# First tile of an attention and low-rank feed-forward block: q's norms wholly on TensorE, v's Gram matrix between q's products, v's low parts ahead of the later scales

## The chip, the cores and the metric

The kernel runs on one core of one Trainium2 chip. The metric is the device time of one launch in microseconds (us). The time before is the median of 3 runs.

## What is computed

x is 4096 rows of 1024 float32. The block is a pre-norm attention whose 32 heads attend to each other within one row, and a feed-forward layer with a low-rank expert part:

```python
q = (layernorm(x) @ wq.T + bq).reshape(B, S, H, D)      # k and v alike; H = D = 32
probs = softmax(einsum('bshd,bstd->bsht', q, k) / sqrt(D))   # 32 x 32 per row
x = x + einsum('bsht,bstd->bshd', probs, v).reshape(B, S, E)
y = layernorm(x)
w_full = softmax of the 2 largest of y @ gate_w.T, on 8 experts
low = einsum('bsd,erd->ebsr', y, lora_A)                 # rank 16
x = x + y @ base_w.T + base_b + 2 * einsum('ebsr,eor,bse->bso', low, lora_B, w_full)
```

All weights are float32 arrays of 1024 x 1024; wq, wk and wv hold values that fp8 can hold. Rows are independent of each other.

## The kernel before

The rows go through in 32 tiles of 128. Every float32 operand of a large product is cut into two float16 parts: the high part is the scaled value rounded to float16, the low part is what is left. A product then is three matmuls (high times high, low rows times high weights, high rows times low weights). From the second tile on, a flag says whether the low parts of k, q and v are zero and the third matmul is left out.

Scaling needs a power of two for each weight matrix before it can be cut. It comes from a norm of the whole matrix: `gram` multiplies each 128-wide column block of each chunk (128 rows of the transposed weight) with itself on TensorE, in bfloat16, 8 matmuls a chunk and 64 a matrix, and adds them up in one PSUM bank. `norm_diag` (VectorE) takes the diagonal, `spread_norm` (TensorE) sums it over the partitions into all of them by a product with ones, and `scale` (VectorE) makes the scale from it in a few instructions of one column. Then `high_parts` (ScalarE, one 128x1024 instruction a chunk) writes the high parts and `split` (VectorE, one a chunk, L1059) the low parts. `attention_scale` and `attention_undo` are short chains on VectorE that need the scales.

In the first tile all of this is interleaved with the tile's own work, in an order written out by hand for each engine:

- SyncE queues the loads: tile 0's rows, the eight chunks of k, the eight of q, k's bias, tile 1's rows, the eight chunks of v (each waits for the low part of the same chunk of k, whose place it takes), the other biases, the expert matrices `ag`, lora_B and the eight chunks of base. q is staged where v's parts will lie, so v's high and low parts wait for the last low part of q.
- TensorE (`first_step`): two chunks of q's Gram matrix, then k's products chunk by chunk (`project_chunk`: 6 matmuls of 512 columns, each waiting for its low part), with one chunk of q's Gram matrix after each of the first three. Only 5 chunks of q go this way (`GRAM_CHUNKS`). `spread_norm("q")` stands before k's last chunk. Then v's Gram matrix, q's products, the Gram matrices of ag, lora and base, the squares of k's low parts, the spreads of these norms, v's products, and the scores (`attend`).
- ScalarE: the high parts of k, the square sums of q's chunks 5 to 7 (`q_norms`, L704), k's bias, the high parts of q, the high part of k's turned rows, the square sums of four low parts of k (`low_part_norms`), the statistics of tile 1's rows, v's high parts 0 to 3, the high part of q's turned rows, v's high parts 4 to 7, `gate_high` (high parts of ag), `normalise_quads(1)` (tile 1's rows are scaled), base's first high parts.
- VectorE: k's low parts, q's scale, q's low parts 0 and 1, the bias adds of k (`add_bias`, L1196, which empty the PSUM banks), `turn_first` (k's rows transposed, L1356), v's scale, q's low parts 2 to 7, `first_low`, v's low part 0, the bias adds of q, `turn_second` (L1369), the diagonals and scales of ag, lora and base, v's low parts 1 to 7, `gate_split`, `turn_quads(1)` (tile 1's rows transposed, L1225), and then the bias adds of v, `turn_third`, `shift` (softmax's maximum) and so on.
- GpSimd: `row_root(1)` (five one-column operations), `second_lo(0)` (low part of q's turned rows, 128x1024, L626), `zero_diag` (four memsets of staged chunks that v's low parts have freed), `v_low(0)` (L632). SyncE spreads k's turned parts into the zeroed diagonal blocks (`first_hi`, `first_lo`).

The engines meet only through semaphores, and each runs its own list in order. Two orders matter for the change: a `norm_diag` on VectorE stands still until the Gram matrix is complete on TensorE, and whatever is behind it in VectorE's list stands with it; and a `project_chunk` on TensorE stands until its low part is there.

Of the kernel before, what the change touches and what calls it, by code (L numbers as in the profile page):

```python
# [69 lines left out]
def block_kernel(nc, x, wT, agT, lora_b, biases, out):  # L70
    T = x.shape[0] // P
    with ExitStack() as ctx:
# [124 lines left out]
        GRAM_CHUNKS = {"k": KC, "q": 5, "v": KC, "ag": KC, "base": KC, "lora": KC}  # L197
# [58 lines left out]
        q_squares = sem("q_squares")  # L256
# [185 lines left out]
        def _(sp):  # L442
# [46 lines left out]
            def first_hi(t):  # L489

                sp.wait_ge(a_hi_ready, t + 1)
                if t > 0:

                    sp.wait_ge(ctx_acc, t)
                else:

                    sp.wait_ge(diag_zero, block_diag_len // HID)
                spread_k(0, t)

            def first_lo(t):  # L500

                sp.wait_ge(a_lo_ready, t + 1)
                spread_k(1, t)
# [196 lines left out]
        def _(act):  # L700
# [5 lines left out]
            def q_norms():  # L706

                for i, k in enumerate(range(GRAM_CHUNKS[SECOND], KC)):
                    act.wait_ge(w_loaded[SECOND][k], 16)
                    if i > 0:  # L710
                        act.wait_ge(q_squares, i)
                    square_sum_of(staged[SECOND][k], norm_in[SECOND][:, P + i:P + i + 1]).then_inc(q_squares, 1)

            def low_part_norms():

                for k in range(LOW_BY_ACT):
                    act.wait_ge(w_lo_done[FIRST], k + 1)
                    act.wait_ge(q_squares, KC - GRAM_CHUNKS[SECOND])
# [67 lines left out]
            q_norms()  # L786
# [53 lines left out]
            def first_step():  # L840
# [3 lines left out]
                low_part_norms()  # L844
# [7 lines left out]
                high_parts("v", w_hi["v"], KC // 2, KC)  # L852
                gate_high()
                normalise_quads(1)
# [134 lines left out]
        def _(dve):  # L989
# [268 lines left out]
            split(FIRST, w_hi[FIRST], w_lo[FIRST], KC - 2, KC)  # L1258
            scale(SECOND)
            attention_scale(1, SECOND)  # L1260
# [160 lines left out]
            def first_step():  # L1421
# [3 lines left out]
                add_bias(0, 1, FIRST, 1, a_acc, a_biased)  # L1425
                norm_diag("v")
                turn_first(0)
# [3 lines left out]
                split(SECOND, w_hi[SECOND], w_lo[SECOND], 2, KC)  # L1431
# [6 lines left out]
                turn_second(0)  # L1438
                norm_diag("ag")
                norm_diag("lora")  # L1440
                norm_diag("base")
                scale("ag")
                scale("lora")
                base_scale()
                split("v", w_hi["v"], w_lo["v"], 1, KC)
# [171 lines left out]
        def _(pe):  # L1617
# [81 lines left out]
            def spread_norm(g):  # L1699

                pe.wait_ge(norm_diags, SCALED.index(g) + 1)
                if GRAM_CHUNKS[g] < KC:

                    pe.wait_ge(q_squares, KC - GRAM_CHUNKS[g])
# [151 lines left out]
            def first_step():  # L1856
# [12 lines left out]
                for k in range(KC):  # L1869
                    if k == KC - 1:  # L1870
                        spread_norm(SECOND)
                    project_chunk(FIRST, k, (0, 1), a_acc)
                    if k + 2 < GRAM_CHUNKS[SECOND]:
# [191 lines left out]
```

## Time and profile before

| | us |
|---|---|
| median of 3 runs | 1277.32 (1276.88 to 1278.81) |
| the profiled execution | 1278.39 |
| its span, first to last instruction | 1275.3 |
| outside the span | 3.1 |
| TensorE busy | 1242.0 (97%) |
| VectorE busy | 1067.5 (84%) |
| ScalarE busy | 743.3 (58%) |
| GpSimd busy | 426.5 (33%) |

The page's 40 slices of 32 us show TensorE at 6, 8 and 9 tenths in the first three and at 9 nearly everywhere after. In the rows, a line gives the start in us from the start of the span, the length in us, the engine, the line of the kernel, the operation, what it writes and reads, and how many instructions are merged; in square brackets stands how long the engine was idle before it and what ended that. PE is TensorE, DVE is VectorE, ACT is ScalarE, POOL is GpSimd. Instructions of one engine overlap a little at their ends, so a merged row's length over its count is close to the distance from one to the next.

### The profile page before, as it was taken

Reading aid. Unit: us, or ns where it says so; the run is one execution under the profiler, and the core shown is the slowest. Engines: PE = TensorE matmul, PEld = TensorE weight load, DVE = VectorE, ACT = ScalarE, POOL = GpSimd, SP = SyncE. Lnnn points to the kernel's source line nnn. Section 1 sums busy time; section 2 is a strip of 40 time slices with the busy share of each in tenths; the row PEclk is TensorE's granted clock in tenths of the full one; section 3 lists DMA queues with packets and bytes.
Section 4 is the critical chain, followed back from the end, with each engine's and each line's share of the span. In section 5 each row is a group of like instructions: output and inputs, shape, how many; then the busy total and the mean of one; then the engine's idle time right before and its main releaser. Section 6 shows DMA issues by size and latency. Waiting matters only on the chain.

```text
span 1275.3 us, 30571 instructions
## 1 busy us (share of the span) xinstructions
PE 1242.0 (97%) x12314; PEld 642.1 (50%) x12314; DVE 1067.5 (84%) x1492; ACT 743.3 (58%) x1149; POOL 426.5 (33%) x340
## 2 busy tenths in 40 slices
PE   6899989999999999999999999999999999999998
PEld 4554445455554545455454555545455555545454
DVE  5799898888888888888888888888888888888886
ACT  4876646665556666555666655566665556666431
POOL 0113433334423333442333344233334423333320
PEclk9999999999999999999999999999999999999999
DMA  9823543344444334444433444443344444333330
GB/s 367 295 67 85 133 100 92 89 101 115 101 96 97 96 84 101 115 101 97 97 96 84 102 115 101 97 96 96 84 103 115 99 98 96 96 84 87 85 84 33
DMA packets 295447, 136.41 MB, mean 107 GB/s; under 512 B 265072, under 2 KB 266096, under 8 KB 295408
## 3 DMA queue, kind: packets, MB, share of 16 engines
q1 hardware_dynamic: 228688, 112.28, 33.6%
q10 hardware_dynamic: 66720, 23.60, 7.8%
q8 instruction: 26, 0.43, 0.1%
q14 instruction: 13, 0.11, 0.0%
HBM read 86.03 MB, written 33.03 MB: 93 GB/s over the span
## 4 chain that ended last, share of the span: by engine, by line
PE 84%; DVE 7%; DMA 3%; issue 2%; ACT 2%; SPq 1%; POOL 0%; DVEq 0%; ACTq 0%
PE acc L1630 23%; PE dense_acc L1790 23%; PE acc L1639 22%; PE attn_ps L1732 7%; PE dense_acc L1800 2%; DMA work<-wT_dram 2%; PE low_ps L1769 1%; PE low_ps L1762 1%; PE low_ps L1763 1%; PE dense_acc L1805 1%; DMA turn_dram<-x_turned 1%; DVE w_lo_k L1059 1%; ACT work L401 1%; DVE work L1196 1%; DVE work L1157 1%
## 5 line engine op out<-in xcount | busy, mean ns | idle before, releaser
L1790 PE MATMUL dense_acc<-base_parts,x 128*128 128x512 f16 x1488 | 331.2, 380 | 1.1 <-issue 1.0
L401 ACT COPY work<-work 32x512 f16<-32x512 f16 x498 | 306.5, 615 | 12.4 <-PE attn_ps L1732 0.3
L1790 PEld LDWEIGHTS dense_acc<-base_parts,x 128*128 128x128 f16 x1488 | 145.7, 99 | 165.6 <-issue 2.2
L632 POOL TENSOR_TENSOR work<-work 128x1024 f16<-128x1024 f32 x32 | 68.4, 2137 | 225.9 <-ACT work L917 225.9
L1196 DVE SCALAR_TENSOR_TENSOR work<-acc,acc_to_a,biases_sb 128x512 f32<-128x512 f32 x192 | 136.3, 738 | 1.8
L582 POOL TENSOR_TENSOR columns<-columns 128x1 f32<-128x1 f32 x31 | 9.1, 293 | 362.9 <-ACT work L797 362.9
L763 ACT CAST x_hi<-x_turned 128x1024 f16<-128x1024 f32 x31 | 32.4, 1044 | 155.3 <-PE acc L1639 154.4
L1630 PE MATMUL acc<-w_hi_k,x_hi 128*128 128x512 f16 x496 | 117.5, 380 | 1.6 <-issue 1.6
L1630 PE MATMUL acc<-v_parts,x_hi 128*128 128x512 f16 x496 | 117.5, 380 | 0.0
L1639 PE MATMUL acc<-w_hi_k,x_lo 128*128 128x512 f16 x496 | 117.2, 379 | 0.0
L1630 PE MATMUL acc<-w_hi_q,x_hi 128*128 128x512 f16 x496 | 117.2, 379 | 0.0
L1639 PE MATMUL acc<-w_hi_q,x_lo 128*128 128x512 f16 x496 | 117.2, 379 | 0.0
L1639 PE MATMUL acc<-v_parts,x_lo 128*128 128x512 f16 x496 | 117.2, 379 | 0.0
L626 POOL TENSOR_TENSOR work<-work 128x1024 f16<-128x1024 f32 x32 | 97.4, 3044 | 47.5 <-ACT work L910 43.5
L1732 PEld LDWEIGHTS attn_ps<-work 128*32 128x32 f16 x6144 | 86.4, 97 | 30.2 <-issue 26.4
L1732 PE MATMUL attn_ps<-work 128*32 128x128 f16 x6144 | 97.5, 220 | 2.9 <-DVE work L1418 1.7
L1307 DVE SCALAR_TENSOR_TENSOR work<-dense_acc,w_undo_bits,work 128x512 f32<-128x512 f32 x64 | 45.2, 747 | 51.7 <-PE dense_acc L1805 48.2
L825 ACT ACTIVATE columns<-columns 128x1 f32<-128x1 f32 x32 | 6.5, 203 | 135.8 <-issue 92.5
L645 POOL TENSOR_TENSOR work<-work,biases_sb 128x1024 f32<-128x1024 f32 x32 | 75.6, 2363 | 17.6 <-DMA out_dram<-work 15.1
L1314 DVE STREAM_TRANSPOSE work<-attn_ps 128x1024 f32<-128x1024 f32 x32 | 63.2, 1975 | 19.4 <-PE attn_ps L1732 19.3
L1639 PEld LDWEIGHTS acc<-w_hi_k,x_lo 128*128 128x128 f16 x496 | 48.4, 98 | 58.8 <-issue 0.5
L1639 PEld LDWEIGHTS acc<-v_parts,x_lo 128*128 128x128 f16 x496 | 48.5, 98 | 58.6
(217 smaller groups left out, 2070.1 us busy)
## 6 DMA issues: line engine op xcount, KB each, us to landing
work<-x_dram SPq DMA_DIRECT2D x64, 512.0 KB, 3.6
work<-work SPq DMA_DIRECT2D x256, 64.0 KB, 2.0
work<-x_dram SPq DMA_DIRECT2D x124, 128.0 KB, 3.8
out_dram<-work SPq DMA_DIRECT2D x31, 512.0 KB, 2.6
x_turned<-turn_dram ACTq DMA_DIRECT2D x30, 512.0 KB, 3.3
work<-wT_dram SPq DMA_DIRECT2D x16, 512.0 KB, 9.9
turn_dram<-x_turned SPq DMA_DIRECT2D x64, 128.0 KB, 3.9
turn_dram<-x_turned ACTq DMA_DIRECT2D x60, 128.0 KB, 4.4
```

Source lines behind the costliest of these rows:

```text
L401: copy(diag[c * QD:(c + 1) * QD, :, c, j::NQ, :], src).then_inc(vdiag_ready, 1)
L626: nc.gpsimd.tensor_tensor(dense_parts[:, :, 1, :], kq_rows(t), dense_parts[:, :, 0, :], ALU.subtract).then_inc(b_lo_ready, 1)
L632: nc.gpsimd.tensor_tensor(v_parts_t[:, :, 1, :], turned3, v_parts_t[:, :, 0, :], ALU.subtract).then_inc(v_lo_ready, 1)
L645: nc.gpsimd.tensor_tensor(biased, h, bias["base"][:, :], ALU.add).then_inc(x1_biased, 1)
L763: nc.scalar.copy(x_hi[:, :, :], x1_turned).then_inc(xhi_ready, 1)
L1196: nc.vector.scalar_tensor_tensor(out=ev[:, s], in0=acc[bank][:, :], scalar=acc_to_a[:, i:i + 1], in1=bias[g][:, s], op0=ALU.mult, op1=ALU. ...
L1307: nc.vector.scalar_tensor_tensor(out=h[:, s], in0=dense_acc[n][:, :], scalar=w_undo[:, BASE_:BASE_ + 1], in1=h[:, s], op0=ALU.mult, op1=AL ...
L1314: nc.vector.transpose(turned.rearrange("p (h d) -> p d h", h=HEADS), attn_ps[:, :].rearrange("p (t d) -> p d t", t=QD)).then_inc(ctx_turne ...
L1630: nc.tensor.matmul(dst, x_hi[:, k, :], w_hi[g][:, k, cols], start=(k == 0), stop=False)
L1639: mm = nc.tensor.matmul(dst, x_lo[:, k, :], w_hi[g][:, k, cols], start=False, stop=(k == KC - 1))
L1732: mm = nc.tensor.matmul(attn_ps[c * QD:(c + 1) * QD, i4 * P:(i4 + 1) * P], dense_parts[:, i, dense_part, :], diag[:, spread_part, :, i, :] ...
L1790: nc.tensor.matmul(dense_acc[n][:, :], rows_part[:, k, :], w_part[:, k, cols], start=(k == 0 and m == 0), stop=False)
```

## The change

TensorE takes over q's last three chunks of norms, and all of q's Gram matrix stands ahead of k's third product chunk; v's Gram matrix is moved from before q's products to between its chunks 1 to 4; base's Gram matrix and the three spreads are moved into the middle of v's products. ScalarE loses `q_norms`, and does `low_part_norms` after v's high parts instead of before the statistics; `gate_high` and `normalise_quads(1)` change places. VectorE does k's last low part after q's scale, q's low parts 2 to 4 ahead of `turn_first` and v's diagonal, 5 and 6 ahead of v's scale, and v's low parts 1 to 3 ahead of the later diagonals, 4 and 5 ahead of the later scales. SyncE's first spread of k's parts waits for two of the four memsets, the second for all four. Nothing after the first tile is edited.

```diff
-        GRAM_CHUNKS = {"k": KC, "q": 5, "v": KC, "ag": KC, "base": KC, "lora": KC}
+        GRAM_CHUNKS = {"k": KC, "q": KC, "v": KC, "ag": KC, "base": KC, "lora": KC}
...
-                    sp.wait_ge(diag_zero, block_diag_len // HID)
+                    sp.wait_ge(diag_zero, block_diag_len // HID // 2)
                 spread_k(0, t)
 
             def first_lo(t):
 
                 sp.wait_ge(a_lo_ready, t + 1)
+                if t == 0:
+                    sp.wait_ge(diag_zero, block_diag_len // HID)
                 spread_k(1, t)
...
             high_parts(FIRST, w_hi[FIRST], 0, KC)
-            q_norms()
             bias_scale(0, FIRST)
...
-                low_part_norms()
                 bias_scale(1, SECOND)
                 row_statistics(1)
                 high_parts("v", w_hi["v"], 0, KC // 2)
...
                 high_parts("v", w_hi["v"], KC // 2, KC)
+                low_part_norms()
+                normalise_quads(1)
                 gate_high()
-                normalise_quads(1)
...
-            split(FIRST, w_hi[FIRST], w_lo[FIRST], KC - 2, KC)
+            split(FIRST, w_hi[FIRST], w_lo[FIRST], KC - 2, KC - 1)
             scale(SECOND)
+            split(FIRST, w_hi[FIRST], w_lo[FIRST], KC - 1, KC)
             attention_scale(1, SECOND)
...
+                split(SECOND, w_hi[SECOND], w_lo[SECOND], 2, 5)
+                turn_first(0)
                 norm_diag("v")
-                turn_first(0)
+                split(SECOND, w_hi[SECOND], w_lo[SECOND], 5, 7)
                 scale("v")
                 attention_scale(2, "v")
                 attention_undo()
-                split(SECOND, w_hi[SECOND], w_lo[SECOND], 2, KC)
+                split(SECOND, w_hi[SECOND], w_lo[SECOND], 7, KC)
...
                 turn_second(0)
+                split("v", w_hi["v"], w_lo["v"], 1, 4)
                 norm_diag("ag")
                 norm_diag("lora")
                 norm_diag("base")
+                split("v", w_hi["v"], w_lo["v"], 4, 6)
                 scale("ag")
                 scale("lora")
                 base_scale()
-                split("v", w_hi["v"], w_lo["v"], 1, KC)
+                split("v", w_hi["v"], w_lo["v"], 6, KC)
...
                 for k in range(KC):
-                    if k == KC - 1:
+                    project_chunk(FIRST, k, (0, 1), a_acc)
+                    if k < 2:
+                        gram(SECOND, 3 * k + 2, 3 * k + 5)
+                    elif k == 2:
                         spread_norm(SECOND)
-                    project_chunk(FIRST, k, (0, 1), a_acc)
-                    if k + 2 < GRAM_CHUNKS[SECOND]:
-                        gram(SECOND, k + 2, k + 3)
-                gram("v", 0, KC)
-                spread_norm("v")
 
                 pe.wait_ge(a_biased, 1)
-                project_chunks(SECOND, (2, 0), b_acc)
+                for k in range(KC):
+                    if k == 5:
+                        spread_norm("v")
+                    project_chunk(SECOND, k, (2, 0), b_acc)
+                    if 1 <= k <= 4:
+                        gram("v", 2 * k - 2, 2 * k)
                 gram("ag", 0, KC)
                 gram_lora()
-                gram("base", 0, KC)
                 square_low_parts(FIRST, LOW_BY_ACT, KC)
-                spread_norm("ag")
-                spread_norm("lora")
-                spread_norm("base")
                 spread_stats(1)
...
-                project_chunks("v", (1, 2), v_acc)
+                for k in range(KC):
+                    if k == 4:
+                        gram("base", 0, KC)
+                        spread_norm("ag")
+                        spread_norm("lora")
+                        spread_norm("base")
+                    project_chunk("v", k, (1, 2), v_acc)
```

## Rows read from the trace of the kernel before

**Rows 1.** The page, first part: busy us, share of the span, instructions

```profile
PE 1242.0 (97%) x12314; PEld 642.1 (50%) x12314; DVE 1067.5 (84%) x1492; ACT 743.3 (58%) x1149; POOL 426.5 (33%) x340
```

**Rows 2.** Stage table: length, busy us (instructions) by engine, granted clock, DMA share, GB/s

```profile
40.00:45.00 5.00, 4.30 (x20) 2.37 (x21) 3.32 (x12) 3.08 (x4) 0.00 (x0) 0.66 1.08 375
```

**Rows 3.** Chain that ended last, first tile: start us, us, what

```profile
30.13 10.14 DMA work<-wT_dram
...
61.77 0.30 DVE w_max L1032
...
70.07 2.39 DVE v_parts L1059 x2
...
73.73 0.37 DVE x_turned L1225
```

**Rows 4.** Timeline, 15 to 34 us, TensorE, VectorE and ScalarE

```profile
16.74 0.63 PE L1661 MATMUL dense_acc<-work 128*128 128x128 bf16 x8 [0.65 <-DMA work<-wT_dram]
...
19.30 0.63 PE L1661 MATMUL dense_acc<-v_parts 128*128 128x128 bf16 x8 [0.57 <-DMA v_parts<-wT_dram]
...
20.25 7.26 DVE L1059 SCALAR_TENSOR_TENSOR w_lo_k<-work,w_scale_bits,w_hi_k 128x1024 f16<-128x1024 f32 x6 [0.52 <-ACT w_hi_k L737]
...
21.59 0.39 PE L1682 MATMUL acc<-w_hi_k,x_hi 128*128 128x512 f16 x1 [1.66 <-DVE w_lo_k L1059]
...
22.89 0.62 PE L1661 MATMUL dense_acc<-v_parts 128*128 128x128 bf16 x8
...
23.36 0.38 PE L1682 MATMUL acc<-w_hi_k,x_hi 128*128 128x512 f16 x1
...
27.31 1.04 ACT L704 ACTIVATE base_parts<-v_parts 128x1024 bf16<-128x1024 f32 x1
...
33.17 8.43 ACT L737 ACTIVATE w_hi_q<-v_parts,w_scale_bits 128x1024 f16<-128x1024 f32 x8 [1.20 <-DVE w_scale_bits L1038]
```

**Rows 5.** Timeline, 36 to 59 us, the same engines

```profile
36.84 1.41 DVE L1196 SCALAR_TENSOR_TENSOR work<-acc,acc_to_a,biases_sb 128x512 f32<-128x512 f32 x2
...
41.56 1.92 DVE L1356 STREAM_TRANSPOSE work<-work 128x1024 f32<-128x1024 f32 x1
...
43.34 0.23 DVE L1032 TENSOR_REDUCE w_max<-dense_acc 128x1 f32<-128x128 f32 x1
...
45.33 7.26 DVE L1059 SCALAR_TENSOR_TENSOR w_lo_q<-v_parts,w_scale_bits,w_hi_q 128x1024 f16<-128x1024 f32 x6
...
52.89 4.26 ACT L737 ACTIVATE v_parts<-work,w_scale_bits 128x1024 f16<-128x1024 f32 x4
...
54.13 1.29 DVE L1059 SCALAR_TENSOR_TENSOR v_parts<-work,w_scale_bits,v_parts 128x1024 f16<-128x1024 f32 x1 [0.39 <-ACT v_parts L737]
...
56.77 2.04 DVE L1369 STREAM_TRANSPOSE work<-work 128x1024 f32<-128x1024 f32 x1
```

**Rows 6.** Timeline, 58 to 75 us

```profile
58.85 0.28 DVE L1025 TENSOR_TENSOR base_parts<-attn_ps,ident 128x128 f32<-128x128 f32 x1
...
59.97 2.13 POOL L626 TENSOR_TENSOR work<-work 128x1024 f16<-128x1024 f32 x1 [3.95 <-ACT work L850]
...
64.01 8.45 DVE L1059 SCALAR_TENSOR_TENSOR v_parts<-work,w_scale_bits,v_parts 128x1024 f16<-128x1024 f32 x7
...
74.81 1.37 DVE L1196 SCALAR_TENSOR_TENSOR work<-acc,acc_to_a,biases_sb 128x512 f32<-128x512 f32 x2
```

**Rows 7.** Timeline, 78 to 89 us

```profile
79.52 2.13 POOL L632 TENSOR_TENSOR work<-work 128x1024 f16<-128x1024 f32 x1 [10.83 <-ACT work L917]
...
80.62 2.11 DVE L1059 SCALAR_TENSOR_TENSOR base_parts<-lora_up,w_scale_bits,base_parts 128x1024 f16<-128x1024 f32 x1
...
83.29 1.22 DVE L1231 TENSOR_TENSOR x_lo<-x_turned,x_hi 128x1024 f16<-128x1024 f32 x1
...
85.01 1.89 PE L1630 MATMUL acc<-w_hi_k,x_hi 128*128 128x512 f16 x8
...
88.98 0.49 PE L1710 MATMUL dense_acc<-columns,low 128*128 128x128 f32 x2 [0.17 <-DVE columns L1124]
```

More of the change, by code:

```diff
@@ L255, in block_kernel @@
         gram_done = sem("gram_done")
-        q_squares = sem("q_squares")
         low_squares = sem("low_squares")
@@ L704, in square_sum_of @@
                 return nc.scalar.activation(square_scratch, part, ACT.Square, accum_out=total)
[L706 to L712, printed above, removed]
             def low_part_norms():
@@ L717, in low_part_norms @@
                     act.wait_ge(w_lo_done[FIRST], k + 1)
-                    act.wait_ge(q_squares, KC - GRAM_CHUNKS[SECOND])
                     if k > 0:
@@ L1701, in spread_norm @@
                 pe.wait_ge(norm_diags, SCALED.index(g) + 1)
-                if GRAM_CHUNKS[g] < KC:
-                    pe.wait_ge(q_squares, KC - GRAM_CHUNKS[g])
                 nc.tensor.matmul(norm_ps[g], ones[:, :], norm_in[g], start=True, stop=True).then_inc(norm_spread, 1)
```

## The prediction

> **What bounds the kernel now.** I read the page first: TensorE is busy for 97% of the span [rows 1], so after the first tile the kernel runs at TensorE's pace, and a first tile that ends d us later ends the whole d us later unless something takes it up. Next the chain that ended last, over the first tile [rows 3]: up to 40.3 us it hangs on the weight loads (v's last chunk lands at 30.13 + 10.14 = 40.27). From there it is VectorE's list nearly all the way: v's scale, q's low parts, the scales of ag, lora and base (from 61.77), v's low parts (the last two at 70.07) and `turn_quads` at 73.73. The last look was the timeline of each engine, for the length of each step and the idle time before it [rows 4 to 7]. At 74.81 VectorE begins to empty v's banks [rows 6]; I measure the change by when that instruction comes.
>
> **What TensorE and the loads allow at the start.** Chunks land 1.28 us apart: from k's last (16.74) to q's second (19.30) are two steps [rows 4]. So q's last lands at 16.69 + 8 x 1.28 = 26.9. A chunk of products takes 22.89 - 21.59 = 1.30 us, a chunk of a Gram matrix 23.36 - 22.89 = 0.47 [rows 4] (64 matmuls 3.7). In the new order TensorE does k's chunk 0, q's Gram chunks 2 to 4, k's chunk 1 (till 25.6) and Gram chunks 5 to 7, the last when it has landed, till 27.4. Then six chunks of products and one spread (0.2): 27.4 + 7.8 + 0.2 = 35.4. Here q's norms, hidden under ScalarE before, delay k's products; they ended at about 33.6.
>
> **q's scale.** Before, ScalarE took the three squares (from 27.31) and began q's high parts at 33.17 [rows 4]. Taken out are 3 squares: between 27.31 and 33.17 lie 1.20 idle and a bias of about 1.13, so they cost 3.53 / 3 = 1.2 each. Now VectorE takes the diagonal at 27.6, does k's low part 6 till 29.1, and q's scale (spread at 28.7 to 29.1) is there at 29.8: 3.4 us earlier. q's high parts then run 29.8 to 38.3 and never bind again. VectorE: k's low part 7 till 31.0, the attention scale, q's low parts 0 and 1 till 34.2 (7.26 / 6 = 1.21 each [rows 4]), and it stands till k's first bank is full. That is one half chunk before the end, 34.9.
>
> **v's scale.** VectorE: bias adds 1.41 [rows 5], q's low parts 2 to 4 (3.63), `turn_first` (1.85, from 1.92 [rows 5]): 34.9 + 6.95 = 41.85. There `norm_diag("v")` waits for the Gram matrix. TensorE may start q's products after the first bias add, 35.75, and does five chunks of products and eight of the Gram matrix: 35.75 + 6.5 + 3.7 + 0.15 for the last one's end = 46.1. So VectorE stands 4.2 us, with q's low part 5 and all else behind it, and TensorE's chunk 5 in turn waits for that low part. This is the wait that takes the place of the loads' (before: till 40.3). Then diagonal 0.27, low parts 5 and 6 2.42 (48.8), scale and attention scales 45.33 - 43.34 = 1.99 [rows 5] (50.8), low part 7 (52.0). Before, q's last low part ended at 45.33 + 7.26 = 52.5 (less an overlap of 0.07). All that the earlier scale gave is 0.5 us.
>
> **Up to q's turned rows.** v's high part 0 may start now at 52.1; before it started at 52.89, since ScalarE was still at the statistics that now come earlier [rows 5]. From there to v's low part 0 took 1.24 (54.13), and from that to the end of `turn_second` 58.65 - 54.13 = 4.52. New: 52.1 + 1.24 + 4.52 = 57.87, which is 0.8 us early.
>
> **v's low parts and the later scales.** Before, from 58.65 VectorE did the three diagonals (0.28 each [rows 6]), waited twice, and made the scales from 61.77 to 64.01, 2.24 us [rows 3, 6]; then seven low parts in 8.45, and 2.42 for `gate_split` and `turn_quads` (from 72.39 to 74.81) [rows 6]. Now low parts 1 to 3 start at 57.87. TensorE, with q's products, ag, lora and the squares done by 56.7, does v's chunks 0 to 3 as these come, and only then base's Gram matrix. VectorE stands at `norm_diag("base")` for that whole row: the last low part, one chunk of products (1.30), 3.7 and 0.17 for the end.
>
> The low parts have a neighbour they did not have. `second_lo(0)` on GpSimd started 1.32 us after `turn_second` had ended, at 59.97, when VectorE had only small instructions [rows 6]; now it comes at 59.2 between low parts 2 and 3. The nearest row for that is base's first low part at 80.62: 2.11 us long, where the others take 1.28; `v_low` ran on GpSimd from 79.52 to 81.65, and the low part ended 1.1 after it [rows 7]. So the low part stood until GpSimd had read its inputs. The bounds: nothing, if GpSimd is the one to wait until VectorE's row of low parts is over; 2.05 us, if it gets in before low part 3. I take the second, because GpSimd arrives while low part 2 runs and stands next.
>
> The Trainium skill has a rule on this ("SBUF — State Buffer", section "SBUF: two separate sides"): a VectorE instruction with two inputs in SBUF and a GpSimd instruction that reads SBUF exclude each other, and whichever starts first holds the port for its whole length. The trace agrees at 80.62. By the rule, 2.05 us are to be paid or nothing, by who comes next, and not a share of it.
>
> The sum: low part 3 ends at 57.87 + 3.63 + 2.05 = 63.55; products and Gram matrix 63.55 + 1.30 + 3.67 + 0.17 = 68.7; diagonal 0.27 and two low parts 2.42: 71.4; scales 2.24: 73.6; two low parts: 76.0; 2.42 for the gate and `turn_quads`: 78.4. That is 78.4 - 74.81 = **3.6 us later**. Without GpSimd it is 1.7 to 1.8.
>
> **What costs nothing.** ScalarE's `low_part_norms` (4 x 1.2) now stands after v's high parts, from about 64.3 to 69.2; `normalise_quads` and `gate_high` follow and are done near 73, as an estimate from the rows' lengths of one 128x1024 instruction, 1.05 [rows 4]. Their cover is that VectorE wants them only at 76.0; had VectorE not waited, they would be late by 1 us or so. SyncE's first spread may go after two memsets, GpSimd does these by about 64.3 and all four by 66.2, so the scores find their operands well before v's products end at 77.3. Moved waits on SyncE hold back only loads with over 9 us of queue ahead of them [rows 3]. Loads of tile 1's quads come earlier and land behind base's.
>
> **Does it reach the end?** Tile 1's first products began at 85.01, when `x1_low(1)` (83.29 + 1.22 = 84.5) and TensorE's squares (84.9) were done together; the next step, at 88.98, waited for VectorE's flag [rows 7]. TensorE's own list would come 2 us later than before, VectorE's 3.6, and the flag at 88.98 takes all of VectorE's delay. After it TensorE has no slack to give back. So 3.6 us: the profiled execution's 1278.39 would become 1282.0. The median of the runs shown is 1.07 below the profiled one; from it I predict 1277.32 + 3.6 = **1280.9 us**.
>
> **The rivals.**
> - GpSimd doesn't get in between the low parts (or gets in where VectorE stands anyway): +1.8, 1279.1. For it: between 53 and 57 small GpSimd operations ran beside a low part of 1.29 [rows 5]. Against it: 80.62.
> - The delay is taken up between 75 and 89 us, where TensorE's and VectorE's lists were equally late [rows 7], or the wait for v's Gram matrix is shorter: 0 to +1, about 1277.8. Against it: both lists come later.
> - TensorE falls to half clock. The granted clock was 0.66 in 40 to 45 us, 1.2 instead of 2.4 GHz for about 3.4 us, after four thin Gram chunks had come with the loads [rows 2]. If the pauses for q's last chunks bring it at 26 us, k's products lose half of 3.4: +1.7 on top, 1282.6. Against it: the pauses are shorter, and 16 to 21.6 us were thin without it.
> - Faster: VectorE doesn't stand at `norm_diag("base")`. The three diagonals then cost 0.8 and the sum is 61.5 + 0.8 + 4.84 + 2.24 + 2.42 = 71.8, 3.0 us early: 1274.3. It decides at one point: base's Gram matrix must be complete when low part 3 is, at 61.5. Its loads have landed by then, but TensorE's order puts v's chunk 3 first, so only a much quicker TensorE could do it.
>
> **Chances and range.** The forecast 0.52; GpSimd out of the way 0.24; taken up 0.07; the clock 0.09; faster 0.08. What a measurement of this kernel can tell from no change is about 0.2%, 2.55 us, so the borders are 1274.8 and 1279.9. Faster has 0.08. Within 0.2% are the second and third case and 0.07 of the forecast (a sum under by 1 us): 0.38. Slower is the rest, 0.54. The forecast's own spread is 1 us either way, for some thirty steps of 1 us with ends known to 0.05. The range is 1277.0 to 1283.6: from the case that is taken up to the clock's case with its spread; it leaves out the faster case and some of the edges, about 0.15.
>
> **What would show it.** In the timeline after: ScalarE has 3 squares fewer and q's high parts begin near 29.8; k's products end near 35.4; VectorE stands about 4 us ahead of v's diagonal, near 42 to 46; `turn_second` ends near 57.9; one of v's low parts 2 or 3 is about 3.3 us long and `second_lo` runs beside it; VectorE stands about 5 us ahead of base's diagonal; the adds of v come near 78.4. If VectorE's wait for base's diagonal is under 2 us, the prediction is wrong. If the low parts all take 1.28, it is the second case.

## The result and the profile after

The changed kernel takes 1280.44 us (median of 20 runs, 1278.54 to 1284.18) beside 1277.31 for the kernel before (20 runs, 1275.91 to 1280.41): a ratio of 1.0025 with a 95% interval of 1.0019 to 1.0032, or 3.1 us more (2.4 to 4.1). The profiled execution took 1279.5, its span is 1277.6.

A time also holds what lies outside the span, and that part differs between the two programs: 1.8 to 1.9 us in each of these 20 executions of the changed kernel, and 2.1 to 4.0 with a median of 2.4 in the 57 of the kernel before that were timed beside the experiments. So the time shows about 0.5 us less than the span loses. In the two profiled executions the difference is larger: 1.1 us in the time (1278.39 and 1279.49), 2.3 in the span, 1.2 outside. Why it differs stays open.

From the page of the changed kernel, the line that answers to [rows 1]:

```profile
PE 1242.1 (97%) x12338; PEld 643.2 (50%) x12338; DVE 1067.7 (84%) x1492; ACT 740.7 (58%) x1143; POOL 427.9 (33%) x340
```

TensorE's work is the same (1242.1 us, before 1242.0), so the difference is idle time of TensorE. First where it arises. The timeline of the changed kernel over the first tile, all engines mixed, in the columns of [rows 4]:

```profile
21.80 0.61 PE L1678 MATMUL acc<-w_hi_k,x_hi 128*128 128x512 f16 x1 [1.56 <-DVE w_lo_k L1050]
...
24.34 1.62 PE L1657 MATMUL dense_acc<-v_parts 128*128 128x128 bf16 x24
...
28.67 0.29 DVE L1016 TENSOR_TENSOR base_parts<-dense_acc,ident 128x128 f32<-128x128 f32 x1 [0.94 <-PE dense_acc L1657]
...
30.89 8.42 ACT L729 ACTIVATE w_hi_q<-v_parts,w_scale_bits 128x1024 f16<-128x1024 f32 x8 [1.55 <-DVE w_scale_bits L1029]
...
36.01 1.41 DVE L1187 SCALAR_TENSOR_TENSOR work<-acc,acc_to_a,biases_sb 128x512 f32<-128x512 f32 x2 [0.87 <-PE acc L1680]
...
47.17 0.29 DVE L1016 TENSOR_TENSOR base_parts<-dense_acc,ident 128x128 f32<-128x128 f32 x1 [4.26 <-PE dense_acc L1657]
...
58.90 5.48 DVE L1050 SCALAR_TENSOR_TENSOR v_parts<-work,w_scale_bits,v_parts 128x1024 f16<-128x1024 f32 x3
...
60.21 3.09 POOL L627 TENSOR_TENSOR work<-work 128x1024 f16<-128x1024 f32 x1 [9.12 <-ACT work L840]
...
69.61 0.29 DVE L1016 TENSOR_TENSOR base_parts<-dense_acc,ident 128x128 f32<-128x128 f32 x1 [4.84 <-PE dense_acc L1657]
...
79.26 1.37 DVE L1187 SCALAR_TENSOR_TENSOR work<-acc,acc_to_a,biases_sb 128x512 f32<-128x512 f32 x2
```

In the square brackets stand the two large waits: 4.26 us ahead of v's diagonal (47.17, line 1016) and 4.84 us ahead of base's (69.61). Between them v's low parts 1 to 3 take 5.48 us for three (58.90), where seven took 8.45, 1.2 each [rows 6]; `second_lo` (60.21, GpSimd) runs beside them and is 3.09 us long instead of 2.13 [rows 6]. VectorE begins to empty v's banks at 79.26; before it was at 74.81 [rows 6]: 4.45 us later.

The kernel before had waits of its own in this stretch of VectorE's list, ahead of v's diagonal, of base's, and of the scale of ag:

```profile
41.35 0.29 DVE L1025 TENSOR_TENSOR base_parts<-dense_acc,ident 128x128 f32<-128x128 f32 x1 [3.11 <-PE dense_acc L1661]
...
59.70 0.29 DVE L1025 TENSOR_TENSOR base_parts<-dense_acc,ident 128x128 f32<-128x128 f32 x1 [0.57 <-PE dense_acc L1661]
...
61.77 0.29 DVE L1032 TENSOR_REDUCE w_max<-dense_acc 128x1 f32<-128x128 f32 x1 [1.77 <-PE dense_acc L1705]
```

With 0.39 ahead of v's first low part [rows 5] they are 5.84 us between k's adds and v's. In the changed kernel they are 4.26, 0.21 and 4.84, and 1.9 more go into the longer low parts: 11.2. That is 5.4 more, and the way from k's adds to v's adds grew by 5.3 (from 37.97 to 43.25); k's adds themselves come 0.83 earlier. So the waits and the longer low parts account for the whole delay.

One thing in this list I had not put in the forecast: q's diagonal comes at 28.67, 1.1 us after its forecast. The stage table of the changed kernel (columns as in [rows 2]):

```profile
20.00:25.00 5.00, 3.44 (x20) 1.55 (x18) 4.54 (x4) 5.00 (x6) 0.00 (x0) 0.55 1.02 406
25.00:30.00 5.00, 5.00 (x56) 3.66 (x54) 4.06 (x5) 3.78 (x4) 0.00 (x0) 1.00 1.02 408
```

Over 20 to 25 us TensorE was granted 0.55 of its clock, so it ran at 1.2 GHz nearly throughout; from 25 us on it had 2.4 GHz. k's first chunk of products, begun at 21.80, took till the next Gram chunks began at 24.34: 2.5 us instead of 1.30.

Then where it goes. The same instruction of each tile, `shift`, starts 4.4 to 4.6 us later in tiles 0 to 2, and 2.3 us later from tile 3 on, to the end. Timelines of the kernel before, ScalarE's exponentials at tile 1 and `shift` of tile 3 and of the last tile:

```profile
155.60 1.15 ACT L922 ACTIVATE work<-work,columns 128x1024 f32<-128x1024 f32 x1 [2.39 <-DMA turn_dram<-x_turned]
...
196.57 1.22 DVE L1389 TENSOR_REDUCE top<-attn_ps 128x32 f32<-128x1024 f32 x1 [0.27 <-PE attn_ps L1732]
...
1238.26 1.22 DVE L1389 TENSOR_REDUCE top<-attn_ps 128x32 f32<-128x1024 f32 x1 [0.21 <-PE attn_ps L1732]
```

and of the changed kernel:

```profile
159.20 1.15 ACT L913 ACTIVATE work<-work,columns 128x1024 f32<-128x1024 f32 x1 [1.36 <-DVE work L1386]
...
198.93 1.22 DVE L1381 TENSOR_REDUCE top<-attn_ps 128x32 f32<-128x1024 f32 x1 [0.28 <-PE attn_ps L1725]
...
1240.53 1.23 DVE L1381 TENSOR_REDUCE top<-attn_ps 128x32 f32<-128x1024 f32 x1 [0.21 <-PE attn_ps L1725]
```

From 196.57 to 198.93 are 2.36 us, from 1238.26 to 1240.53 are 2.27: after tile 3 nothing is lost or won any more. Of the 2.2 us won back between tiles 2 and 3, 1.0 stands in the first rows: before, ScalarE waited 2.39 us behind the transfer of the turned rows, after only 1.36, and then for VectorE. The rest may go with TensorE's clock: the granted clock over 190 to 195 us was 0.66 in this profile of the kernel before and 1.00 in the one of the changed kernel. So the pair of profiles shows two things that a second pair must confirm (below).

### The profile page after: what moved, and what is told of

It reads as the page before. It is cut to its first block, busy times and chain, and to the rows that moved or that the text cites. A ratio compares the mean times of both kernels' runs of the same rounds, so it can differ in the third digit from the quotient of the medians.

```text
span 1277.6 us, 30612 instructions
## 1 busy us (share of the span) xinstructions
PE 1242.1 (97%) x12338; PEld 643.2 (50%) x12338; DVE 1067.7 (84%) x1492; ACT 740.7 (58%) x1143; POOL 427.9 (33%) x340
## 4 chain that ended last, share of the span: by engine, by line
PE 84%; DVE 7%; issue 3%; DMA 3%; ACT 2%; SPq 1%; POOL 0%; DVEq 0%; ACTq 0%
PE acc L1626 23%; PE dense_acc L1783 22%; PE acc L1635 22%; PE attn_ps L1725 6%; PE dense_acc L1793 2%; DMA turn_dram<-x_turned 1%; PE low_ps L1762 1%; PE low_ps L1755 1%; PE low_ps L1756 1%; PE dense_acc L1798 1%; PE dense_acc L1657 1%; DMA work<-wT_dram 1%; DVE work L1187 1%; DVE v_parts L1050 1%; ACT work L400 1%
```

## The experiments

The theory: 4.45 us come from VectorE's two waits and from the port that a low part has to leave to GpSimd, as forecast, plus about 1.1 us of half clock in the new order of TensorE. The rivals are that one of these isn't there, or is paid back before tile 1. The parts may add up to more than 4.45, since the changed kernel's waits take the place of those that the kernel before had (5.84 us). I undid each by itself. Every ratio is to runs of the kernel before on the same chip; the first four experiments ran on one chip, the next four on another, so a time of one group is compared with one of the other only by these ratios. Where an experiment's profile is set beside the changed kernel's, I first bring both to the same start at q's diagonal, since the clock moves that one (27.4 to 30.3) and every later step with it.

**The changed kernel once more.** No edit.

> The changed kernel as it is, timed beside the next three and looked at once more. Its first profile had TensorE at half clock from 21.8 to about 24.5 us, k's first product chunk took 2.74 us instead of 1.30, and everything up to v's adds came 1.0 to 1.1 later than I had worked out (79.26 us instead of 78.4); only 2.3 us of those 4.45 were left at the end of the span. If the half clock is a matter of chance, this profile shows k's first chunk at 1.3 us or at 2.7, and v's adds near 78.2 or near 79.3; if it is a property of the new order, it shows 2.7 and 79.3 again. Time: 1.0025 of the kernel before.

Measured: 1280.14 us beside 1277.94, ratio 1.0019 (1.0009 to 1.0028). Its timeline:

```profile
28.69 0.29 DVE L1016 TENSOR_TENSOR base_parts<-dense_acc,ident 128x128 f32<-128x128 f32 x1 [1.27 <-PE dense_acc L1657]
...
58.93 5.46 DVE L1050 SCALAR_TENSOR_TENSOR v_parts<-work,w_scale_bits,v_parts 128x1024 f16<-128x1024 f32 x3
...
79.27 1.37 DVE L1187 SCALAR_TENSOR_TENSOR work<-acc,acc_to_a,biases_sb 128x512 f32<-128x512 f32 x2
```

Step by step it is the first profile again, half clock included (granted clock 0.68 over 20 to 25 us). Of both measurements the change costs some 2.2 to 3.1 us. This is the profile that I compare the others with.

**GpSimd's low part only after v's low parts 1 to 3.**

```diff
                 row_root(1)
+                pool.wait_ge(w_lo_done["v"], 4)
                 second_lo(0)
```

> The changed kernel, with GpSimd's second_lo(0) waiting for v's low part 3, so that it reads SBUF when VectorE stands at base's diagonal. Theory (the port is held for the whole instruction): low parts 1 to 3 take 3.65 us instead of 5.48, base's diagonal comes 1.85 us earlier, v's adds near 77.4 instead of 79.3, and the kernel is 1.0 to 1.9 us faster than the changed one (as much as half may be taken up in tiles 2 and 3, as in the first profile). Rival (the long low parts came from something else, or TensorE's order sets the time): low parts 5.5 us again, no gain.

Measured: 1279.33 us, ratio 1.0015 (1.0007 to 1.0024). Timeline, VectorE and GpSimd:

```profile
27.64 0.29 DVE L1017 TENSOR_TENSOR base_parts<-dense_acc,ident 128x128 f32<-128x128 f32 x1
...
57.88 3.60 DVE L1051 SCALAR_TENSOR_TENSOR v_parts<-work,w_scale_bits,v_parts 128x1024 f16<-128x1024 f32 x3
...
61.56 2.14 POOL L627 TENSOR_TENSOR work<-work 128x1024 f16<-128x1024 f32 x1 [11.49 <-DVE v_parts L1051]
...
66.92 0.29 DVE L1017 TENSOR_TENSOR base_parts<-dense_acc,ident 128x128 f32<-128x128 f32 x1 [5.04 <-PE dense_acc L1658]
...
76.56 1.37 DVE L1188 SCALAR_TENSOR_TENSOR work<-acc,acc_to_a,biases_sb 128x512 f32<-128x512 f32 x2
```

The three low parts take 3.60 instead of 5.46, 1.86 less, and `second_lo` is 2.14 long again. VectorE's wait for base's diagonal grows by 0.21: a low part takes 1.2 and a chunk of products 1.30, so TensorE falls a little behind VectorE. v's adds come 2.71 earlier; 1.05 of it is the earlier start (27.64 against 28.69), and 1.66 are left, which is 1.86 - 0.21 but for the rounding. So the port's price in the trace is shown: 1.9 at the low parts, 1.7 at v's adds. In the time it is 0.8, with intervals that overlap.

**Base's Gram matrix back where it was.**

```diff
                 gram_lora()
+                gram("base", 0, KC)
                 square_low_parts(FIRST, LOW_BY_ACT, KC)
...
                     if k == 4:
-                        gram("base", 0, KC)
```

> The changed kernel with base's Gram matrix back ahead of the squares and of v's products, the three spreads and VectorE's order as changed. Theory (VectorE's stand at base's diagonal costs most): the Gram matrix is complete at about 59 us when base's last chunk has landed, VectorE doesn't stand at the diagonal (4.84 us before), v's products start at 61 and run without a gap, v's adds come at 74.6 instead of 79.3, and the kernel is 2.3 to 4.6 us faster than the changed one, so between level with the kernel before and 2 us faster than it. Rival (TensorE's later start on v's products costs as much as VectorE's stand): v's adds at 78 or later, no gain.

Measured: 1277.47 us, ratio 0.9997 (0.9988 to 1.0006). Timeline of VectorE:

```profile
29.42 0.29 DVE L1016 TENSOR_TENSOR base_parts<-dense_acc,ident 128x128 f32<-128x128 f32 x1 [1.92 <-PE dense_acc L1657]
...
65.52 0.28 DVE L1016 TENSOR_TENSOR base_parts<-dense_acc,ident 128x128 f32<-128x128 f32 x1
...
74.25 1.35 DVE L1062 SCALAR_TENSOR_TENSOR ag_lo<-base_parts,w_scale_bits,ag_hi 128x1088 f16<-128x1088 f32 x1 [1.43 <-ACT ag_hi L742]
...
76.68 1.37 DVE L1187 SCALAR_TENSOR_TENSOR work<-acc,acc_to_a,biases_sb 128x512 f32<-128x512 f32 x2
```

The diagonal at 65.52 waits for nothing. But `gate_split` at 74.25 now waits 1.43 us for ScalarE's high parts of ag. That is the cover which the prediction named and priced: without VectorE's wait, `low_part_norms` ahead of `gate_high` makes ScalarE late "by 1 us or so". 4.83 - 1.43 = 3.4 should be gained, and the trace has 3.3 (79.27 - 76.68, and 0.73 for the later start). In the time it is 2.7, and the whole loss is gone. Undone alone, this is the largest single cause at v's adds; in the time it can't be told from the next one, since the intervals overlap.

**v's Gram matrix in two blocks after q's chunks 0 and 1.**

```diff
-                    if 1 <= k <= 4:
-                        gram("v", 2 * k - 2, 2 * k)
+                    if k == 0:
+                        gram("v", 0, 5)
+                    elif k == 1:
+                        gram("v", 5, KC)
```

> The changed kernel with v's Gram chunks 0 to 4 after q's product chunk 0 and 5 to 7 after chunk 1, instead of two after each of chunks 1 to 4. Theory (VectorE stands 4.26 us at v's diagonal because TensorE is late with the matrix): it is complete at about 43 us instead of 47, VectorE doesn't stand there, turn_second ends near 55 instead of 58.9; but v's low parts wait less and base's Gram matrix still waits for low part 3, so v's adds come near 75.4: 2 to 3.9 us faster than the changed kernel. Rival (ScalarE's high parts of q or the loads bind first, or base's diagonal takes the gain back since the loads of base land at 58): less than 1 us.

Measured: 1277.92 us, ratio 1.0003 (0.9994 to 1.0012). Timeline of VectorE:

```profile
27.55 0.29 DVE L1016 TENSOR_TENSOR base_parts<-dense_acc,ident 128x128 f32<-128x128 f32 x1 [0.77 <-PE dense_acc L1657]
...
42.17 0.29 DVE L1016 TENSOR_TENSOR base_parts<-dense_acc,ident 128x128 f32<-128x128 f32 x1 [0.36 <-PE dense_acc L1657]
...
46.28 0.29 DVE L1023 TENSOR_REDUCE w_max<-dense_acc 128x1 f32<-128x128 f32 x1 [1.43 <-PE dense_acc L1698]
...
75.78 1.36 DVE L1187 SCALAR_TENSOR_TENSOR work<-acc,acc_to_a,biases_sb 128x512 f32<-128x512 f32 x2
```

The wait for v's diagonal is 0.36 instead of 4.26. Not all of it arrives: v's scale at 46.28 waits 1.43 for the spread, which TensorE still does ahead of q's chunk 5. From 3.9 less, 2.35 is left at v's adds (79.27 - 75.78 = 3.49, of which 1.14 is the earlier start). In the time it is 2.2.

**Six matmuls of 512 columns where TensorE would wait for k's first low part.** They write to a bank that k's first matmul then overwrites.

```diff
                 gram(SECOND, 0, 2)
+                for k in range(6):
+                    nc.tensor.matmul(acc[0][:, :], x_lo[:, k, :], x_hi[:, 0:4, :].rearrange("p k n -> p (k n)"),
+                                     start=True, stop=True)
```

> The changed kernel with six more matmuls of 512 columns on TensorE between q's Gram chunk 1 and k's first products (their result is overwritten), where it stands for 1.6 us before. In three of the profiles of the new order (the first, its repeat, and the one with base's Gram matrix put back) TensorE was at half clock from about 21 to 24 or 25 us, in two (GpSimd later, v's Gram matrix early) it wasn't; q's diagonal came at 28.7, 28.7 and 29.4 us with it and at 27.6 without. Theory (a thin stretch ahead of k's products, of which the new order has no slack to absorb the cost): no half clock there, q's diagonal at 27.6, v's adds near 78.2 instead of 79.3, the time 0.5 to 1 us shorter than the changed kernel's and less scattered. Rival (the half clock is set off by something else, such as the stretch of loads before 20 us): half clock again, or no change of the time.

Measured: 1279.43 us, ratio 1.0013 (1.0004 to 1.0022). The stage table:

```profile
20.00:25.00 5.00, 4.64 (x46) 2.97 (x44) 5.00 (x5) 5.00 (x6) 0.00 (x0) 1.00 1.02 406
```

and the timeline, TensorE and VectorE:

```profile
18.80 1.46 PE L1863 MATMUL acc<-x_hi,x_lo 128*128 128x512 f16 x6
...
27.36 0.29 DVE L1016 TENSOR_TENSOR base_parts<-dense_acc,ident 128x128 f32<-128x128 f32 x1 [0.82 <-PE dense_acc L1657]
...
77.95 1.37 DVE L1187 SCALAR_TENSOR_TENSOR work<-acc,acc_to_a,biases_sb 128x512 f32<-128x512 f32 x2
```

With TensorE at work from 18.80 to about 20.3 the clock stays at 2.4 GHz, q's diagonal comes at 27.36, and v's adds 1.32 us earlier for 1.33 at the diagonal: the whole delay is passed on as far as v's adds. Thus the half clock costs 1.0 to 1.3 us there. At the end of this execution nothing of it is left: the last `shift` starts at 1241.64, in the profile beside it at 1240.67, because this one lost 2 us between tiles 2 and 3 (below). The ratios, 1.0013 here and 1.0019 there, have intervals that overlap, so no gain in time is shown.

**Before, with q's part of the change alone.** All of q's Gram matrix on TensorE and ahead, the three squares gone from ScalarE, q's scale between k's last two low parts; the rest as before.

```diff
-        GRAM_CHUNKS = {"k": KC, "q": 5, "v": KC, "ag": KC, "base": KC, "lora": KC}
+        GRAM_CHUNKS = {"k": KC, "q": KC, "v": KC, "ag": KC, "base": KC, "lora": KC}
...
-            q_norms()
...
-                    if k == KC - 1:
-                        spread_norm(SECOND)
                     project_chunk(FIRST, k, (0, 1), a_acc)
-                    if k + 2 < GRAM_CHUNKS[SECOND]:
-                        gram(SECOND, k + 2, k + 3)
+                    if k < 2:
+                        gram(SECOND, 3 * k + 2, 3 * k + 5)
+                    elif k == 2:
+                        spread_norm(SECOND)
...
```

> The kernel before with q's part of the change alone: all of q's norms by TensorE ahead of k's third chunk, no squares of q on ScalarE, k's last low part after q's scale. v's and base's Gram matrices and all low parts of q and v stay in the old order. Theory (the earlier scale of q is worth nothing by itself, since v's last chunk lands at 40.3 us whatever is done before, and the loss comes from v's and base's parts): k's products end near 35.5 instead of 33.6, v's diagonal at 41.4 and v's adds at 74.8 as before, the time within 0.5 us of the kernel before. Rival (q's part costs what k's products are late by, 1.1 to 1.8 us; or it gains, since q's low parts wait less): v's adds off by 1 us or more either way.

Measured: 1275.96 us (1274.31 to 1276.46), ratio 0.9985 (0.9977 to 0.9994). Timeline, TensorE and VectorE:

```profile
36.90 3.85 PE L1656 MATMUL dense_acc<-work 128*128 128x128 bf16 x64
...
40.78 0.29 DVE L1019 TENSOR_TENSOR base_parts<-dense_acc,ident 128x128 f32<-128x128 f32 x1 [2.92 <-PE dense_acc L1656]
...
74.27 1.37 DVE L1190 SCALAR_TENSOR_TENSOR work<-acc,acc_to_a,biases_sb 128x512 f32<-128x512 f32 x2
```

v's Gram matrix now runs in one row behind k's products (36.90, 64 matmuls), no longer chunk by chunk with the loads, and v's diagonal comes at 40.78. Here my expectation failed: the time is 1.5 us less, not within 0.5, and the interval of the ratio leaves out 1. Where the gain arises depends on which profile of the kernel before stands beside it. Beside the first, v's adds come 0.54 us earlier and the last `shift` 1.4, so 0.9 arise between tiles 2 and 3. Beside the second profile (below), v's adds come 1.40 earlier and the last `shift` 1.3, so all of it is in the first tile. That q's part gains is shown; how much of it in the first tile, 0.5 to 1.4, is not settled.

**All three waits taken away.** v's Gram matrix as above, with its spread ahead of q's chunk 3; base's Gram matrix in thirds behind v's chunks 0, 1 and 2; VectorE does v's low parts 1 to 5 ahead of the diagonals and 6 ahead of the scales; ScalarE does two of the low parts' norms earlier and two later; GpSimd does `second_lo` after the memsets and the split of the gate.

```diff
                 row_root(1)
-                second_lo(0)
                 zero_diag()
+                pool.wait_ge(w_lo_done["ag"], 1)
+                second_lo(0)
...
-                split("v", w_hi["v"], w_lo["v"], 1, 4)
+                split("v", w_hi["v"], w_lo["v"], 1, 6)
...
                     if k == 4:
-                        gram("base", 0, KC)
...
                     project_chunk("v", k, (1, 2), v_acc)
+                    if k < 3:
+                        gram("base", 3 * k, min(3 * k + 3, KC))
```

> The changed kernel with the three causes taken out together: v's Gram matrix after q's product chunks 0 and 1 and its spread before chunk 3; base's Gram matrix in thirds after v's chunks 0, 1 and 2; v's low parts 1 to 5 ahead of the later diagonals, 6 ahead of the scales, 7 behind; GpSimd's second_lo(0) after the gate's low part, when VectorE transposes; two of ScalarE's four squares of k's low parts in its stand before v's high parts, the other two after gate_high. Theory (VectorE's stands and the shared port are what the first tile costs): VectorE stands nowhere for over 1 us from 36 us on, low parts 1 to 5 at 1.2 us each, v's adds near 70.5 instead of 79.3 (74.8 before), and the kernel is 3 to 4.5 us faster than the kernel before and 6 or more faster than the changed one. Rival (TensorE or the loads bind as soon as VectorE doesn't, or the lead is taken up in tiles 2 and 3): v's adds at 70.5 but a time within 1.5 us of the kernel before.

Measured: 1271.39 us (1269.75 to 1273.56), ratio 0.9950 (0.9937 to 0.9962). Timeline of VectorE:

```profile
30.31 0.29 DVE L1018 TENSOR_TENSOR base_parts<-dense_acc,ident 128x128 f32<-128x128 f32 x1 [2.28 <-PE dense_acc L1659]
...
63.83 0.29 DVE L1018 TENSOR_TENSOR base_parts<-dense_acc,ident 128x128 f32<-128x128 f32 x1 [0.31 <-PE dense_acc L1659]
...
71.21 1.37 DVE L1189 SCALAR_TENSOR_TENSOR work<-acc,acc_to_a,biases_sb 128x512 f32<-128x512 f32 x2
```

Waits of 3.9 and 4.5 us and 1.86 at the port are gone, 10.3 in all. v's adds come 8.1 us earlier than in the changed kernel, though q's diagonal comes 1.6 later (30.31); from the same start it would be 9.7. Against the kernel before, v's adds are 3.6 us early and the time is 6.1 less, more than the 3 to 4.5 expected. The last `shift` is 5.0 early, as 1.5 are won between tiles 2 and 3; about 0.5 lies outside the span, and the profiled execution (1272.2) is 0.8 above the median.

**The same with the six matmuls.** Edit: the two before together.

> The kernel of the run before with the six matmuls ahead of k's products as well. Theory: at best another 0.5 us on the median, and no half clock before 30 us; v's adds near 70.5 in every case. Rival: the same time.

Measured: 1270.57 us (1268.87 to 1270.89), ratio 0.9945 (0.9932 to 0.9958). This is the fastest version, 7 us (0.55%) under the kernel before. Timeline, VectorE, GpSimd and TensorE:

```profile
27.53 0.29 DVE L1018 TENSOR_TENSOR base_parts<-dense_acc,ident 128x128 f32<-128x128 f32 x1 [0.25 <-PE dense_acc L1659]
...
42.15 0.29 DVE L1018 TENSOR_TENSOR base_parts<-dense_acc,ident 128x128 f32<-128x128 f32 x1 [0.36 <-PE dense_acc L1659]
...
54.35 5.98 DVE L1052 SCALAR_TENSOR_TENSOR v_parts<-work,w_scale_bits,v_parts 128x1024 f16<-128x1024 f32 x5
...
67.42 2.13 POOL L627 TENSOR_TENSOR work<-work 128x1024 f16<-128x1024 f32 x1 [8.47 <-DVE ag_lo L1064]
...
68.42 1.37 DVE L1189 SCALAR_TENSOR_TENSOR work<-acc,acc_to_a,biases_sb 128x512 f32<-128x512 f32 x2
...
69.70 1.52 PE L1727 MATMUL attn_ps<-work 128*32 128x128 f16 x96 [1.55 <-POOL work L627]
```

q's diagonal is 2.78 us earlier than in the run without the six matmuls, v's adds 2.79. In the time it is 0.8, with intervals that overlap; one reason may be that the half clock does not come in every execution (its share in the timed runs is not known). Against the kernel before v's adds are 6.4 us early. The next limit is in the last row: the scores wait 1.55 us for GpSimd's low part, which now comes last.

**The kernel before once more**, no edit, to see what of the first pair of profiles belongs to the program:

> The kernel before, for another profile of the same program. In its first profile TensorE was at half clock at 40 to 44 us and again at 190 to 195 us (about 1 us on tile 3), and the write and fetch of tile 1's turned rows took 6 us near 150, where most of the other profiles have 4 to 5. Theory (the half clock at 40 us belongs to the program, since the stretch before it is thin by the loads; that at 190 us and the slow fetch are chance): half clock at 40 to 44 again, v's adds at 74.8 within 0.2, the other two may be gone, and with them up to 2 us between tile 2 and tile 3. Rival (all of it belongs to the program): the same three again.

Measured: 1277.54 us, a single run. Stage table and then the timeline of VectorE:

```profile
20.00:25.00 5.00, 3.50 (x16) 1.92 (x17) 4.84 (x5) 5.00 (x6) 0.00 (x0) 0.70 1.03 408
...
45.00:50.00 5.00, 4.14 (x12) 1.56 (x13) 5.00 (x5) 4.66 (x10) 0.00 (x0) 0.66 1.03 410
```

```profile
75.67 1.37 DVE L1196 SCALAR_TENSOR_TENSOR work<-acc,acc_to_a,biases_sb 128x512 f32<-128x512 f32 x2
```

Here my expectation failed: the half clock isn't at 40 to 45 us [rows 2] but at 45 to 50, and there is another at 20 to 25, which the first profile of this kernel did not have. So neither belongs to the program in the sense that it comes each time. q's diagonal is at 28.63 here and v's at 40.48, while in the first profile they are at 27.43 and 41.35: the wait for v's loads swallows what the half clock at 20 to 25 us costs. The one at 45 to 50 us is not swallowed: TensorE is later with base's Gram matrix (VectorE waits 1.85 us for it, before 0.57), and v's adds come 0.86 us later than in the first profile, not within 0.2 as expected. So the 4.45 us between the first two profiles are one case of several: with two profiles of the kernel before and three of the changed one, v's adds are 3.6 to 4.8 us apart.

**And the changed kernel a third time.**

> The changed kernel, a third profile. Theory (the half clock at 21 to 25 us is chance, but likely in this order): q's diagonal either at 28.7 or near 27.6, v's adds 79.3 or 78.2, low parts 1 to 3 5.47, VectorE's stands 4.26 and 4.83 in both cases.

Measured: 1281.69 us, a single run. Timeline of VectorE:

```profile
29.01 0.29 DVE L1016 TENSOR_TENSOR base_parts<-dense_acc,ident 128x128 f32<-128x128 f32 x1 [1.25 <-PE dense_acc L1657]
...
79.60 1.37 DVE L1187 SCALAR_TENSOR_TENSOR work<-acc,acc_to_a,biases_sb 128x512 f32<-128x512 f32 x2
```

Half clock again (granted clock 0.76 over 20 to 25 us). In this pair v's adds come 79.60 - 75.67 = 3.9 us later, and the last `shift` 1241.26 - 1238.16 = 3.1.

## Why the prediction was right

**q's scale.** q's high parts were forecast to begin at 29.8 and began at 30.89; k's adds at 34.9 and came at 36.01. Both are 1.1 late by the half clock alone: in the two runs where TensorE kept 2.4 GHz up to there and only GpSimd or the six matmuls differed, q's diagonal came at 27.64 and 27.36 against the forecast 27.6.

**v's diagonal.** The wait was forecast at 4.2 and is 4.26, in six profiles with this order to the hundredth. That it comes from the place of the Gram matrix in TensorE's list is shown by moving that ahead (0.36). (The terms ahead of it, 1.41, 3.63 and 1.85, add up to 6.89 and not 6.95, which changes nothing here.) "All that the earlier scale gave is 0.5 us" is not tested by a run: the one with q's part alone has another order behind k's adds, and its 0.54 is 1.40 beside the second profile of the kernel before.

**v's low parts and the port.** I had chosen 2.05 us for the port over nothing, by the row at 80.62 [rows 7]. Three low parts took 5.48; at 1.2 each that is 1.9 extra, and holding GpSimd back removed 1.86. The choice was right. Only the way in was a little different: `second_lo` began at 60.21 while low part 2 ran, so of its 3.09 us about 1.0 is waiting and 2.1 work, and then low part 3 waited. The Trainium skill says in "SBUF — State Buffer", section "SBUF: two separate sides", that such a pair of instructions exclude each other and the first holds the port for its whole length; these rows agree.

**Base's diagonal.** The wait is 4.84, forecast about 5, and with base's Gram matrix back in its place it is gone. The rival "faster" needed that Gram matrix to be complete when low part 3 was; it was missing by 5 us.

**What costs nothing.** ScalarE's norms were hidden as said, and the price without the cover (1 us or so) was measured at 1.43.

**The sum.** Forecast 3.6 at v's adds; measured 4.45, 3.9 in the second pair. The forecast had v's adds at 78.4, and with TensorE at 2.4 GHz they came at 77.95, so the other terms were together 0.4 too long. The term that was missing is the half clock at 20 to 25 us. I had it as a rival at 0.09, worth 1.7; it was in three of three profiles of the changed kernel and cost 1.0 to 1.3 at v's adds. My reason against it ("16 to 21.6 us were thin without it") was read from one profile of a kernel in which it comes by chance; the second profile of the same kernel has it. In all, it is there in 7 of the 10 profiles without the six matmuls and in neither of the two with them. Nor did it come where the rival put it, at 26 us at the pauses for q's last chunks: the clock fell between 17.4 and 22.7 us (from the granted clock in stretches of 1 us).

**Does it reach the end?** I wrote that TensorE has no slack to give back after 88.98, so that all of the 3.6 us would reach the end. This step failed, though the time came out in the range: of 4.45 us only 2.3 reached the last tile, of 3.9 in the second pair 3.1. I also carried what lies outside the span over unchanged; it was 1.9 us instead of the 3.1 of the profiled execution, about 0.5 less in most. What is taken up lies between tiles 2 and 3. In both profiles of the kernel before, ScalarE's exponentials at tile 1 wait 2.39 and 2.30 us behind the turned rows' transfer; in the three of the changed kernel 1.36, 1.45 and 1.58, and not for the transfer but for VectorE. That is worth 0.7 to 1.0 us. The remainder in the first pair, about 1.0, goes with half clock at 190 to 195 us, which was in one profile of the kernel before and not in the other, so it is chance. All twelve profiles fit these two terms. From `shift` of tile 2 to that of tile 3 are 42.3 to 42.7 us in the seven with neither, 43.3 with the long wait alone (the second profile of the kernel before), 43.55 with the half clock alone (q's part alone, and v's Gram matrix early), and 44.4 and 44.5 with both (the six matmuls, and the first profile of the kernel before). Why the transfer lands later relative to the work in the kernel before stays open: the run with the six matmuls also has 2.48, with the changed order.

So the forecast of +3.6 and the measured +3.1 (2.4 to 4.1) agree partly by luck, because sizes were off in opposite directions: 1.0 to 1.3 too little for the clock, 0.7 to 1.0 too much for what reaches the end, and about 0.5 too much for what lies outside the span. Each of the named waits was of the size forecast.

## What to carry to other kernels

When work is moved ahead in one engine's list, ask what the list then stands at. Here two of the moves, ahead of v's and of base's diagonal, were paid for by waits for Gram matrices that TensorE had been given later. Putting these matrices early in TensorE's list, together with a later low part on GpSimd and ScalarE's norms in another place, turned +3 us into -6, and -7 with the six matmuls. In lists that run in order, look at where the producer stands before the consumer is moved. And a clock seen in one profile is no property of the program: take a second profile of the same kernel before arguing from it.

## What the runs showed of the hardware that I had not expected

- TensorE ran at 1.2 GHz for part or all of 20 to 25 us in 7 of 10 profiles (granted clock 0.50 to 0.77), without ever having stood idle for more than 1.7 us since its first work at 7.5 us: it had come through bursts of 0.6 us every 1.3 us, with pauses for the loads between. For one program it comes and goes: the kernel before had 1.00 and 0.70 there, and 0.66 at 40 to 45 us in one profile and at 45 to 50 in the other. In neither of the two profiles with six more 512-column matmuls at 18.8 us did it come. That they prevent it is not shown. In two profiles (the changed kernel's first, 0.77 over 15 to 20 us, and that with all three waits gone, 0.74) the clock had fallen before 18 us, ahead of their place, so they can't have helped there; and if they did nothing at all, two profiles without it would still come with a chance of about 0.3 x 0.3 = 0.09.
- A GpSimd instruction with two inputs gets the port between two VectorE instructions that follow each other without a pause: it starts during the one, waits about 1.0 us for its end, and then the next one is 1.9 us longer (3.17 instead of 1.28). It was so in all six profiles with that order. GpSimd's memsets did not do that: in the fastest version five low parts took 5.98, 1.2 each, while three of them ran.
